# A mixture-of-experts block: the experts' second activation block is turned by the DMA instead of TensorE

## What is computed

```python
# T = 4096 tokens, D = 512, E = 8 experts, top 2, INTER = 352
h = layernorm(x) * (1 + cb) + sb
scores = sigmoid(h @ gate_w.T)              # top 2 of scores + router_bias, weights normed
h1 = einsum('td,edh->eth', X, W1)
h3 = einsum('td,edh->eth', X, W3)
y = einsum('eth,ehd->etd', silu(h1) * h3, W2)
out = einsum('etd,te->td', y, gate_full)    # gate_full is 0 but for the two chosen experts
out = out + shared                          # two shared experts, as one of width 704
x = x + gb * out
```

## Time and profile before

| | |
|---|---|
| median of 3 runs | 1209.02 us (1205.82 to 1209.89) |
| profiled execution, its own time | 1205.3 us |
| span of the profiled execution | 1203.3 us |
| TensorE busy | 1182.6 us, 98% |
| VectorE, ScalarE, GpSimd busy | 818.0, 430.8, 500.5 us |
| DMA moved | 189.49 MB, mean 157 GB/s |
| granted clock of TensorE | 0.996 |

### The profile page before, as it was taken

How to read it: one execution, slowest core, us unless ns; L and a number is a source line. 1 busy time by engine, 2 the same in 40 slices (tenths; PEclk the granted TensorE clock), 3 DMA queues, 4 the chain that set the end, 5 groups by cost and what they waited for, 6 DMA issues and landing times.

```text
span 1203.3 us, 25592 instructions
## 1 busy us (share of the span) xinstructions
PE 1182.6 (98%) x9012; PEld 775.3 (64%) x9012; DVE 818.0 (68%) x1649; ACT 430.8 (36%) x947; POOL 500.5 (42%) x411
## 2 busy tenths in 40 slices
PE   9999999999999999999999999999999999999996
PEld 5546666666666666767777777756666566656663
DVE  6557778878776777655857754357776777677765
ACT  4334444545443433333323323223332333233331
POOL 2214466657564545222112112335455444554552
PEclk9999999999999999999999999999999999999999
DMA  7725697898787878745534535488888999898873
GB/s 245 226 46 147 150 251 197 212 229 219 188 222 192 227 204 195 174 101 119 126 87 104 135 90 113 95 160 151 144 158 148 147 155 154 137 155 150 152 142 53
DMA packets 271784, 189.49 MB, mean 157 GB/s; under 512 B 205024, under 2 KB 217312, under 8 KB 271660
## 3 DMA queue, kind: packets, MB, share of 16 engines
q1 hardware_dynamic: 238736, 124.92, 45.3%
q0 software_dynamic: 20512, 45.62, 22.5%
q10 hardware_dynamic: 12416, 17.31, 5.1%
HBM read 87.07 MB, written 52.75 MB: 116 GB/s over the span
## 4 chain that ended last, share of the span: by engine, by line
PE 91%; DVE 3%; issue 1%; POOL 1%; ACT 1%; DMA 0%; ACTq 0%; POOLq 0%; DVEq 0%
PE ps_o L91 8%; PE ps_o L93 8%; PE ps_o L92 8%; PE ps_vs L91 7%; PE ps_vs L93 6%; PE ps_vs L92 6%; PE ps_vh L91 4%; PE ps_vh L92 4%; PE ps_vh L93 4%; PE ps_kh L91 4%; PE ps_kh L92 4%; PE ps_kh L93 4%; PE ps_qh L91 4%; PE ps_qh L93 4%; PE ps_qh L92 4%; PE ps_y L91 2%
## 5 line engine op out<-in xcount | busy, mean ns | idle before, releaser
L511 POOL DMA_INDIRECT out<-y,slot_row x71 | 132.8, 1870 | 189.8 <-DVE y L981 153.6
L93 PE MATMUL ps_o<-w_all,xt 128*128 x568 | 177.5, 313 | 0.0
L92 PE MATMUL ps_o<-w_all,xt 128*128 x568 | 177.5, 312 | 0.0
L91 PE MATMUL ps_o<-w_all,xt 128*128 x568 | 177.4, 312 | 0.0
L973 DVE SCALAR_TENSOR_TENSOR gate_row<-gate_rows,batch_weight,gate_row 128x512 f32<-128x512 f32 x213 | 159.8, 750 | 14.3 <-ACT gate_row L1274 11.7
L431 POOL DMA_INDIRECT out<-s_sum,row_no x32 | 53.7, 1677 | 197.2 <-DVE s_sum L699 191.6
L91 PE MATMUL ps_qh<-ht,wqkv 128*128 128x128 f16 x512 | 87.5, 219 | 0.8 <-DVE wqkv L667 0.8
L956 DVE SCALAR_TENSOR_TENSOR a<-ps_o,a 128x352 f32<-128x352 f32 x71 | 37.3, 525 | 74.5 <-PE ps_o L93 69.6
L93 PE MATMUL ps_qh<-ht,wqkv 128*128 128x128 f16 x512 | 87.5, 219 | 0.0
L92 PE MATMUL ps_qh<-ht,wqkv 128*128 128x128 f16 x512 | 87.5, 219 | 0.0
L387 POOL TENSOR_TENSOR h<-cen,rows_f 128x512 f32<-128x512 f32 x31 | 39.5, 1275 | 109.7 <-ACT cen L1020 104.4
(11 more groups left out here) (276 smaller groups left out, 3335.6 us busy)
## 6 DMA issues: line engine op xcount, KB each, us to landing
w_stage<-in_w_d ACTq DMA_DIRECT2D x64, 176.0 KB
xb<-in_x SPq DMA_DIRECT2D x32, 256.0 KB, 3.8
xr<-in_x SPq DMA_DIRECT2D x32, 256.0 KB, 4.2
out<-x SPq DMA_DIRECT2D x32, 256.0 KB, 3.7
h_d<-hl SPq DMA_DIRECT2D x32, 256.0 KB, 2.5
h2t_d<-h2t SPq DMA_DIRECT2D x32, 256.0 KB, 3.5
s_ht<-h2t_d SPq DMA_DIRECT2D x32, 256.0 KB, 3.7
wmod<-in_wmod_d SPq DMA_DIRECT2D x12, 512.0 KB, 5.9
```

The lines of the kernel that those rows point to most:

```text
L91: nc.tensor.matmul(out, lh, rh, start=first, stop=False, skip_group_check=True)
L92: nc.tensor.matmul(out, lh, rl, start=False, stop=False, skip_group_check=True)
L93: return nc.tensor.matmul(out, ll, rh, start=False, stop=last, skip_group_check=True)
L511: pool.indirect_dma_start(m.out, bass.IndirectOffsetOnAxis(ap=m.slot_row[:, t:t + 1], axis=0), m.y[:, t % Y_RING, :], None, compute_op=ALU ...
```

## The change

The second block of `a` (columns 128 to 255) goes the way of the third, for tiles 0 to 67. TensorE turns only the first block. `a_rows` gets twice the columns and becomes four separate buffers, two of them in the place of `s_h3c`, a buffer of the shared expert that is free by then. `at_d` holds four blocks (high of blocks 1 and 2, low of blocks 1 and 2) and `at_p` two (high and low of block 0). `e_down` waits for the DMA ahead of its second block instead of its third. In the last three tiles TensorE turns all three blocks, as before, and the copies out of PSUM are cut as 128 and 256 columns instead of 256 and 128.

```diff
@@ sync_program
-            sp.dma_start_transpose(m.at_d[t % ROWS_RING][:, :, :], m.a_rows[:, t % ROWS_RING, :, :].rearrange("p s n -> p (s n)")).then_inc(m.at_loaded[t % 2], 16)
+            sp.dma_start_transpose(m.at_d[t % ROWS_RING][:, :, :], m.a_rows[t % ROWS_RING][:, :, :].rearrange("p s n -> p (s n)")).then_inc(m.at_loaded[t % 2], 16)
@@ e_low_rows
-            v.tensor_tensor(m.a_rows[:, t % ROWS_RING, 1, :], m.a[:, t % 2, 2 * P:IT * P], m.a_rows[:, t % ROWS_RING, 0, :], ALU.subtract).then_inc(m.e_act, 1)
+            v.tensor_tensor(m.a_rows[t % ROWS_RING][:, 1, :], m.a[:, t % 2, P:IT * P], m.a_rows[t % ROWS_RING][:, 0, :], ALU.subtract).then_inc(m.e_act, 1)
@@ e_low
-        v.tensor_tensor(m.at_p[t % HALF_RING][:, 1, :, :], m.ps_a[:, 0:2, :], m.at_p[t % HALF_RING][:, 0, :, :], ALU.subtract).then_inc(m.e_at_lo, 1)
+        v.tensor_tensor(m.at_p[t % HALF_RING][:, 1, :], m.ps_a[:, 0, :], m.at_p[t % HALF_RING][:, 0, :], ALU.subtract).then_inc(m.e_at_lo, 1)
         if t >= BY_DMA:
-            v.tensor_tensor(m.at_d[t % ROWS_RING][:, 1, :], m.ps_a[:, 2, :], m.at_d[t % ROWS_RING][:, 0, :], ALU.subtract).then_inc(m.e_at_lo, 1)
+            v.tensor_tensor(m.at_d[t % ROWS_RING][:, 2:4, :], m.ps_a[:, 1:IT, :], m.at_d[t % ROWS_RING][:, 0:2, :], ALU.subtract).then_inc(m.e_at_lo, 1)
@@ e_high_rows
-            act.activation(m.a_rows[:, t % ROWS_RING, 0, :], m.a[:, t % 2, 2 * P:IT * P], ACT.Copy).then_inc(m.e_silu, 1)
+            act.activation(m.a_rows[t % ROWS_RING][:, 0, :], m.a[:, t % 2, P:IT * P], ACT.Copy).then_inc(m.e_silu, 1)
@@ e_high
-        act.activation(m.at_p[t % HALF_RING][:, 0, :, :], m.ps_a[:, 0:2, :], ACT.Copy).then_inc(m.e_at_hi, 1)
+        act.activation(m.at_p[t % HALF_RING][:, 0, :], m.ps_a[:, 0, :], ACT.Copy).then_inc(m.e_at_hi, 1)
         if t >= BY_DMA:
-            act.activation(m.at_d[t % ROWS_RING][:, 0, :], m.ps_a[:, 2, :], ACT.Copy).then_inc(m.e_at_hi, 1)
+            act.activation(m.at_d[t % ROWS_RING][:, 0:2, :], m.ps_a[:, 1:IT, :], ACT.Copy).then_inc(m.e_at_hi, 1)
@@ e_turn
-        for k in range(2 if t < BY_DMA else IT):
+        for k in range(1 if t < BY_DMA else IT):
@@ e_down
-            if k < 2:
-                turned = (m.at_p[t % HALF_RING][:, 0, k, :], m.at_p[t % HALF_RING][:, 1, k, :])
+            if k == 0:
+                turned = (m.at_p[t % HALF_RING][:, 0, :], m.at_p[t % HALF_RING][:, 1, :])
             else:
-                turned = (m.at_d[t % ROWS_RING][0:w, 0, :], m.at_d[t % ROWS_RING][0:w, 1, :])
-                if t < BY_DMA:
+                turned = (m.at_d[t % ROWS_RING][0:w, k - 1, :], m.at_d[t % ROWS_RING][0:w, k + 1, :])
+                if t < BY_DMA and k == 1:
                     pe.wait_ge(m.at_loaded[t % 2], ring_use(t, 2))
@@ place_buffers
-    m.at_p = [(sb, late_halves, late_halves)[j](f"at_p{j}", [P, 2, 2, P], F16) for j in range(HALF_RING)]
-    m.at_d = [late_halves(f"at_d{j}", [P, 2, P], F16) for j in range(ROWS_RING)]
-    m.a_rows = region(ACT_AT, AT_AT)("a_rows", [P, ROWS_RING, 2, P], F16)
+    act_rows, h3c_rows = region(ACT_AT, AT_AT), region(H3C_AT, W_STAGE_AT)
+    m.at_p = [sb(f"at_p{j}", [P, 2, P], F16) for j in range(HALF_RING)]
+    m.at_d = [late_halves(f"at_d{j}", [P, 4, P], F16) for j in range(ROWS_RING)]
+    m.a_rows = [(act_rows, act_rows, h3c_rows, h3c_rows)[j](f"a_rows{j}", [P, 2, 2 * P], F16) for j in range(ROWS_RING)]
```

More of the change, by code:

```diff
@@ L1707, in place_buffers @@
     m.passed = sb("passed", [1, SLOT_TILES, E], F32)
-    GATE_AT, ACT_AT, AT_AT, UP_BYTES = SHARED_AT + 8192, SHARED_AT + 12288, SHARED_AT + 14336, UP_COLS * 2
+    GATE_AT, ACT_AT, AT_AT, H3C_AT, UP_BYTES = SHARED_AT + 8192, SHARED_AT + 12288, SHARED_AT + 14336, SHARED_AT + 24576, UP_COLS * 2
     staged, third, second = region(W_STAGE_AT, W_AT), region(SHARED_AT, SHARED_AT + 4096), region(SHARED_AT + 4096, SHARED_AT + 8192)
```

## The result

| | before | after |
|---|---|---|
| median of the runs | 1205.9 us (1204.9 to 1209.9, 6 runs) | 1198.9 us (1197.3 to 1201.4, 6 runs) |
| profiled execution, its own time | 1205.3 us | 1200.9 us |
| span | 1203.3 us | 1198.9 us |

The ratio is 0.9943, 95% interval 0.9932 to 0.9954: 7.0 us faster. The three runs shown ahead of the prediction had a median of 1209.0, and with three more it is 1205.9. The forecast of 1201.5 is 2.6 us above the measured 1198.9: the base was 3.1 us too high, and the gain is 7.0 us instead of 7.5. What tests the forecast's mechanism is the gain.

The account below looks back on a forecast made before the run. TensorE was taken to bound the kernel. 68 transposes at 0.11 us take 7.5 us from the profiled 1205.3, giving 1197.8; the runs' median lies 3.7 higher, giving 1201.5 us, range 1196.5 to 1208; ScalarE, VectorE, SP and DMA count nothing.

Parts of the forecast that it names:

- What bounds: Routed experts, from about 785 us on: TensorE busy 100.00 of 100 us, 91% of the chain of waits.
- The price of one transpose: TensorE, tiles 0 to 67: 0.11 us each, between 0.08 and 0.14; 68 give 7.5 us, between 5.4 and 9.5.
- ScalarE and VectorE: Rows work doubles to 256 columns, about 407 and 414 ns; `y` about 0.2 us later; nothing on the sum.
- SP's issue time: SP's queue: issue time hardly depends on size, so 0; single issues up to 2.3 us as the other end.
- The room of the turned block: Ahead of `e_down`'s second block: 6.1 us left in the tightest tile, transfer 0.5 us longer, costed at nothing.
- the rival on late blocks: Turned block late in single tiles, by 1 us in five or six: 2 us of gain left, 1207; chance 0.10.
- the signs that I had named for being wrong: TensorE waits before the DMA's buffer, windows under 99 of 100, later issues tile after tile, or beat 5.7 us and above.
- The DMA as the bound: Rival, routed experts: DMA sustaining only 149 GB/s makes a tile 6.2 us, adding 29 us: 1238; chance 0.09.
- The point of decision: DMA rate of 160 GB/s, below which the change loses; a beat of 5.63 us needs 163 GB/s.
- The forecast's number: Median 1201.5 us, from 1209.0 before; own range 1199.5 to 1203.6, or down to 1196.5 with the lower group of runs.
- the rival with every transfer on the path: Turned block's latency on the path in each tile: at least 83 us added, 1288; chance 0.01.
- The rule against the change: Skill's 390 ns on TensorE against 1309 ns by DMA: would lose 0.9 us a tile, some 60 us.

Follow-up runs that it names:

- the second run: The change run once more as it is, with its own profile: 1198.0 us, ratio 0.9944 to the kernel before.
- three tiles ahead: Gathered rows' transpose issued three tiles ahead on SP's queue instead of four: change 1197.95 us, kernel before 1205.4 us, all three blocks by the DMA 1190.8 us.
- four tiles ahead: Gathered rows' transpose issued four tiles ahead on SP's queue, as in the change (1198.0 us run again); with all three blocks by the DMA 1195.4 us.

## Why the prediction was right

- **What bounds.** TensorE alone, in every tile. Taking 68 instructions from it, with nothing else touched, gave the full 7.5 us.
- **The price of one transpose.** Taken as 0.11 us from two distances between starts. The three measurements are 7.5/68 = 0.110, 7.0/68 = 0.103 and 14.4/136 = 0.106, the last with an interval of 0.093 to 0.122 by its ratio. The ends of 0.08 (a weight load that nothing covers) and 0.14 did not come: a single transpose shows 0.11 in the timeline. Its weight load takes 139 to 141 ns by the record and still runs beside its neighbour.
- **ScalarE and VectorE.** No effect on the sum, as forecast. `y` came 0.24 us later, as forecast with 0.2, and nobody waited.
- **SP's issue time.** It hardly depends on the size, as forecast: 1.17 us at the least for 64 KB, 1.19 for 128 KB, 1.21 for 192 KB. The other end, 2.3 us for a single issue, was set too low: one took 3.22 in the change, and the one of tile 11 took 2.23 and so used 1 us of its room.
- **The room of the turned block: the one weak step.** I costed it at nothing, from 6.1 us of room in the tightest tile and 0.5 us more of transfer, and bounded the transfer from above with 6.8 us by the absence of waits. That bound has a fault: a tile without a wait bounds its own transfer by its own room, and only the tightest tile had as little as 6.8. In the changed kernel the transfer of tile 10 took 7.5 us from the end of its issue (8.8 from its start), and nobody waited. In tile 11 the transfer, 6.6 us from the end of the issue, was inside the bound. What broke there was the room, 3.7 us instead of 6.1, since the issue was 4.4 us late instead of 3.4 and took 2.23 us instead of 1.19. It cost 2.8 us. This is the mechanism of the rival on late blocks, in one tile instead of five or six, and it left the verdict as it was. Two of the signs that I had named for being wrong appeared with it, a wait ahead of the first matmul on the DMA's buffer and a window under 99 of 100, and I had not said how many tiles it takes for them to count.
- **The DMA as the bound.** The point of decision was put at 160 to 163 GB/s, from the traffic of the stage, with the remark that what is moved is what is asked for. The remark was the right half: 165 GB/s in two stages of the change and then 180 in all three with every block on the DMA went through without a wait. The forecast of 8.5 points more share was worth little as well. It rose by 20, 11 and 3 points in the three stages, and in the profile of the second run the last stage has 0.93, 2 points less than before, at 162 GB/s.
- **The forecast's number.** The base of 1209.0 us was a median of three, two of them the slowest of six. The range had allowed for the lower group of runs and so took in the measured time, but it is too wide to prove anything: the kernel before, with its median of 1205.9 over six runs, lies inside it as well. What bears the forecast out is the gain, the beat and the runs above. The low end of 1196.5 is 0.2 above what its own terms give (1199.5 - 3.2), and the time of the rival with every transfer on the path, 1288, starts from the profiled 1205.3 where the others start from 1209. Neither touches the forecast.
- **The rule against the change.** A transpose on TensorE costs 0.11 us of path here, and the DMA's version 2.5 to 9 us from issue to landing. The Trainium skill ("VectorE: DVE Perf Modes", section "The three transpose paths") gives 390 and 1309 ns for the two, for bf16, and its rules for authors prefer TensorE. The trace agrees that the DMA is the slower way, and with neither figure. The choice went the other way, because TensorE's 0.11 us stood on the path and the DMA's microseconds did not.

## What to carry to other kernels

Where one engine is busy without a gap, price an instruction by the distance between starts. If the result is wanted only long after, a slower route that stands off the path can take the work. Then look at the queue of that route: a DMA that waits for its input holds everything behind it, so put first what is wanted first. Judge the room against the worst issue delay and the worst landing together, not against one profile's tightest tile.

## What was new about the hardware

- The landing time of the transposing DMA hardly follows its size. With three tiles ahead, min/median/max are 2.3/3.9/5.9 us for the 64 KB of the turned rows in the kernel before and 2.6/4.0/5.7 for the 128 KB in the change. The 256 KB of the gathered rows take 3.1/3.8/5.9 in the same profile of the change, and 3.1/4.3/6.2 with all three blocks by the DMA. For the 192 KB of that kernel the profile gives no landing. What does move it is the order of SP's queue: with four tiles ahead, the 128 KB have 9.0 as their longest. By which way the order does this is not shown. The kernel with 64 KB, in its profile with three tiles ahead:

```profile
L362 SPq DMA_TRANSPOSE at_d<-a_rows x68: 1168/1170/1206, 787.2 to 1169.3; - x68
...
DMA to landing us min/median/max: 2.3/3.9/5.9
```

- SP's issue is often longer when it follows another at once. In the change the 32 issues of the turned rows that came within 0.3 us of another's end took 1.50 us in the median and up to 3.22, the 33 that came 0.3 to 2 us behind one 1.20. It is not so each time: the issue at 860.31, 0.1 us behind another, took 1.22. With three tiles ahead no issue of the turned rows follows at once, and their median is 1.19. Those of the gathered rows, which now all do, have 1.33, where the kernel before has 1.24.
- A DMA share of 1.05 to 1.07 over 300 us went with no wait of TensorE for a transfer. The kernel with only the transpose taken out moves what the kernel before moves, and its share in the last of the three stages is 0.98 beside 0.95. So the share is no measure of what is left.
